# Time mixing of an RWKV layer: the gap of key and top, and the residual of the shift product, summed in PSUM by identity products

## The reference, cut to what matters

```
xs = shift x by one token;  xk = x*tm_k + xs*(1-tm_k)   (xv, xr likewise)
k = xk @ Wk.T;  v = xv @ Wv.T;  r = sigmoid(xr @ Wr.T)
per token t and channel (w: decay, u: time_first):
    q   = max(pp, k + u)
    e1  = exp(pp - q);  e2 = exp(k + u - q)
    wkv = (e1*aa + e2*v) / (e1*bb + e2)
    pp_new = max(pp - exp(w), k);  aa, bb carried on
out = x + (r * (layernorm(wkv)*ln_g + ln_b)) @ Wo.T
```

## Time and profile before

| | |
|---|---|
| median of 3 runs | 853.4 us (853.35 to 854.92) |
| the profiled execution | 852.91 us, its span 851.2 us |
| busy over the span | PE 649.4 us, PEld 534.9, DVE 541.4, ACT 342.6, POOL 327.1 |
| the time mixing's phase | from 447.3 to 617.7 us of the span |
| mean granted clock of PE | 0.878 of full speed |

### The profile page before, as it was taken

The page is one execution under the profiler, slowest core; times in us unless marked ns, Lnnn a source line. Parts: engine busy times, 40 slices in busy tenths (PEclk is TensorE's granted clock), DMA queues, the critical chain, the costliest instruction groups (busy, mean ns, idle before and its releaser), DMA issues. The chain is left out here.

```text
span 851.2 us, 14119 instructions
## 1 busy us (share of the span) xinstructions
PE 649.4 (76%) x4265; PEld 534.9 (63%) x4265; DVE 541.4 (64%) x1122; ACT 342.6 (40%) x760; POOL 327.1 (38%) x306
## 2 busy tenths in 40 slices
PE   4989999669916999999944899999344069999600
PEld 3656665358815888888833788888344048888400
DVE  4578989626782556444421799998556748888433
ACT  1567777324402333333315566544045025555200
POOL 5877764000003343434314466634310043331075
PEclk9999999969967999999986999999755569999855
DMA  4000000045303111111106000000059023332154
GB/s 124 1 2 1 2 2 2 3 149 189 95 1 87 52 56 57 57 57 50 50 25 198 1 1 1 2 0 1 0 180 307 8 67 98 99 100 81 50 152 138
DMA packets 38466, 54.23 MB, mean 64 GB/s; under 512 B 7252, under 2 KB 30422, under 8 KB 38262
## 3 DMA queue, kind: packets, MB, share of 16 engines
q1 hardware_dynamic: 31624, 34.80, 12.7%
q0 software_dynamic: 6768, 18.49, 7.3%
HBM read 37.28 MB, written 15.99 MB: 63 GB/s over the span
## 5 line engine op out<-in xcount | busy, mean ns | idle before, releaser
L1611 PE MATMUL banks<-r_xt,r_w_mixed 128*128 128x256 f32 x384 | 86.6, 385 | 1.4 <-ACT r_xt L1679 1.4
L1611 PEld LDWEIGHTS banks<-r_xt,r_w_mixed 128*128 128x128 f32 x384 | 73.1, 192 | 12.4 <-ACT r_xt L1679 2.1
L1357 DVE SCALAR_TENSOR_TENSOR f0x_s<-f0x_th,banks 128x512 f32<-128x512 f32 x35 | 24.1, 689 | 82.7 <-ACT f0x_th L1316 78.0
L1219 POOL DMA_INDIRECT f_y<-f0x_yout,f_slot_of x35 | 34.4, 983 | 102.1 <-ACT f0x_yout L1335 99.9
L1205 POOL DMA_INDIRECT f1x_xg<-f_xn,f_token_of x39 | 37.0, 948 | 75.5 <-PE banks L1256 50.9
L568 DVE TENSOR_REDUCE a_ssum<-a_e 128x6 f32<-128x1536 f32 x32 | 56.0, 1749 | 2.7 <-ACT a_e L454 2.5
L1272 PE MATMUL banks<-f_w_hi,f0x_xt_hi 128*128 x140 | 56.1, 401 | 0.2 <-issue 0.2
L1316 ACT ACTIVATE f0x_th<-banks 128x512 f32<-128x512 f32 x35 | 20.9, 598 | 86.5 <-PE banks L1272 86.5
L1272 PE MATMUL banks<-f_w_hi,f0x_xt_lo 128*128 x140 | 55.6, 397 | 0.0
L1272 PE MATMUL banks<-f_w_lo,f0x_xt_hi 128*128 x140 | 55.3, 395 | 0.0
L454 ACT ACTIVATE a_e<-banks 128x1536 f32<-128x1536 f32 x32 | 46.5, 1455 | 15.8 <-PE banks L351 15.8
(11 more groups left out here) (330 smaller groups left out, 1889.0 us busy)
## 6 DMA issues: line engine op xcount, KB each, us to landing
f_y<-f1x_yout SPq DMA_DIRECT2D x39, 128.0 KB
f0r_stage<-in_f_w13T SPq DMA_DIRECT2D x4, 1024.0 KB
r_y<-f_y SPq DMA_DIRECT2D x16, 256.0 KB, 6.0
f1r_stage<-in_f_w13T SPq DMA_DIRECT2D x8, 512.0 KB
f0r_stage<-in_f_w2T SPq DMA_DIRECT2D x4, 512.0 KB
f_xn<-f0r_xn SPq DMA_DIRECT2D x8, 256.0 KB
f1r_stage<-in_f_w2T SPq DMA_DIRECT2D x8, 256.0 KB
f_xn<-f1r_xn SPq DMA_DIRECT2D x8, 256.0 KB
```

The source lines that it names most:

```text
L1219: pool.indirect_dma_start(k.y_dram, bass.IndirectOffsetOnAxis(ap=k.slot_of[:, t:t + 1], axis=0), yout[:, t % YB, :], None).then_inc(scatte ...
L1611: last = pe.matmul(bank(1 + kind)[:, eb * T:(eb + 1) * T], r.w_mixed[:, kind, j // KB, j % KB, eb * P:(eb + 1) * P], xt[:, b % 2, j % KB, ...
```

## The change: what it does

Two sums that DVE did are made by PE in PSUM, as products with an identity matrix.

- The gap. `ku` and `dif` are gone. PE gets a step `gap(b)`, between `centre(b-1)` and `shift(b-1)`: for each half, k times the identity and top times minus the identity (`less_one`) are accumulated in bank 5, 4 products in all. It waits for `top_done(b)`. `clamp(b)` on ACT now reads bank 5, in halves, with `first` (u) as bias, or minus u (`less_first`) where the scale is -1: 4 instructions of 128 x 256 in place of 2 of 128 x 512. The two `ku` instructions of ACT and the one `dif` of DVE go.
- The residual. `shift(b-1)` adds x_res times the identity to each of its two groups, 2 products more. `add_shift(b-1)` moves from DVE to ACT: a Copy of bank 7 into x_res, no addition.
- Bank 5 is also where `deviate` writes, so `deviate(b-1)` also waits for `rel_done(b)`.
- DVE makes `less_one` (128 x 128) and `less_first` (128 x 2) once, in the expert phase before.

```
+  less_one = ident * -1;  less_first = first * -1          # DVE, once, in prepare(0)
 PE
+  def gap(self, b):
+      pe.wait_ge(done["top_done"], b + 1)
+      at_least(pe, done["ve_done"], b - 1)
+      for eb in range(EB):
+          pe.matmul(bank(5)[:, eb * T:(eb + 1) * T], m.ident[:], kt[:, 0, eb, 0:T], start=True, stop=False)
+          last = pe.matmul(bank(5)[:, eb * T:(eb + 1) * T], r.less_one[:], top[:, eb, 0:T], start=False, stop=True)
+      last.then_inc(done["dif_in"], 1)
   def shift(self, b):
+      pe.wait_ge(done["added"], b + 1)
       for s in range(S):
           for eb in range(EB):  pe.matmul(bank(7)..., s1..., r.wo_shift...)
+          last = pe.matmul(bank(7)[:, s * D:(s + 1) * D], m.ident[:], m.x_res[:, S * b + s, :],
+                           start=False, stop=True)
   def deviate(self, b):
+      pe.wait_ge(done["rel_done"], min(b + 2, B))
 ACT
   def products(self, b):
-      for eb in range(EB):
-          last = act.activation(ku[:, eb, :], bank(1)..., ACT.Identity, bias=r.first[:, eb:eb + 1])
+  def add_shift(self, b):
+      act.wait_ge(done["shifted"], b + 1)
+      act.activation(m.x_res[:, S * b:S * b + S, :], bank(7)..., ACT.Copy).then_inc(done["shift_added"], 1)
   def clamp(self, b):
-      act.activation(rel[:, 0], dif[:], ACT.Relu)
-      act.activation(rel[:, 1], dif[:], ACT.Relu, scale=-1.0).then_inc(done["rel_done"], 1)
+      for eb in range(EB):
+          act.activation(rel[:, 0, eb, :], gap, ACT.Relu, bias=r.first[:, eb:eb + 1])
+          last = act.activation(rel[:, 1, eb, :], gap, ACT.Relu, bias=r.less_first[:, eb:eb + 1], scale=-1.0)
 DVE
-  def gap(self, b):        dve.tensor_tensor(dif[:], ku[:], top[:, :, 0:T], ALU.subtract)
-  def add_shift(self, b):  dve.tensor_tensor(two, two, bank(7)..., ALU.add)
```

More of the change, by code:

```diff
@@ L1396, in prepare @@
                     dve.tensor_scalar(r.grown[:], r.grown[:], -1.0, None, ALU.mult)
+                    dve.tensor_scalar(r.less_one[:], m.ident[:], -1.0, None, ALU.mult)
+                    dve.tensor_scalar(r.less_first[:], r.first[:], -1.0, None, ALU.mult)
                 elif 1 <= n <= 3 * KB:
@@ L1464, in rwkv_memory @@
     r.mean_of, r.cen_same, r.cen_other = sb("mean_of", [P, P]), sb("cen_same", [P, P]), sb("cen_other", [P, P])
+    r.less_one, r.less_first = sb("less_one", [P, P]), sb("less_first", [P, EB])
     return r
@@ L1478, in rwkv_phase @@
     xt = sb("xt", [P, 2, KB, T + 1])
-    kt, ku, vs = sb("kt", [P, 2, EB, T + 1]), sb("ku", [P, EB, T]), sb("vs", [P, EB, T])
+    kt, vs = sb("kt", [P, 2, EB, T + 1]), sb("vs", [P, EB, T])
     th, s1 = sb("th", [P, EB, T]), sb("s1", [P, 2, EB, T])
     less, sc, ab = sb("less", [P, 2, EB, T]), sb("sc", [P, 3, EB, T]), sb("ab", [P, 2, EB, T + 1])
-    dif, rel, ex = sb("dif", [P, EB, T]), sb("rel", [P, 2, EB, T]), sb("ex", [P, 2, EB, T])
+    rel, ex = sb("rel", [P, 2, EB, T]), sb("ex", [P, 2, EB, T])
     e2v, e1a, num, den, rden, wkv, sq, rw = (
@@ L1487, in rwkv_phase @@
     names = ("edges first_weighed second_weighed first_added added stats_done mv_done ve_in_done root_done neg_mean_ready "
-             "xn_ready xt_in_psum xt_ready r_done k_done v_done th_done s1_done k_ready ku_ready v_ready "
-             "top_done less_done sc_done dif_done rel_done ex_done f2v_done e2v_done scan_done e1a_done num_done "
+             "xn_ready xt_in_psum xt_ready r_done k_done v_done th_done s1_done k_ready v_ready "
+             "top_done less_done sc_done dif_in rel_done ex_done f2v_done e2v_done scan_done e1a_done num_done "
              "e1b_done den_done rden_done wkv_done centred sq_done rw_done shifted shift_added var_done ve_done rstd_done "
@@ L1606, in products @@
                 pe.wait_ge(done["xt_ready"], b + 1)
-                for kind, free, made in ((2, "th_done", "r_done"), (0, "ku_ready", "k_done"), (1, "v_ready", "v_done")):
+                for kind, free, made in ((2, "th_done", "r_done"), (0, "k_ready", "k_done"), (1, "v_ready", "v_done")):
                     at_least(pe, done[free], b)
@@ L1631, in shift @@
                     for eb in range(EB):
-                        last = pe.matmul(bank(7)[:, s * D:(s + 1) * D], s1[:, b % 2, eb, s * P:(s + 1) * P],
-                                         r.wo_shift[:, eb, :], start=(eb == 0), stop=(eb == EB - 1))
+                        pe.matmul(bank(7)[:, s * D:(s + 1) * D], s1[:, b % 2, eb, s * P:(s + 1) * P],
+                                  r.wo_shift[:, eb, :], start=(eb == 0), stop=False)
+                    last = pe.matmul(bank(7)[:, s * D:(s + 1) * D], m.ident[:], m.x_res[:, S * b + s, :],
+                                     start=False, stop=True)
                 last.then_inc(done["shifted"], 1)
@@ L1691, in products @@
                 at_least(act, done["less_done"], b)
+                at_least(act, done["dif_in"], b)
                 act.activation(k_in, bank(1).rearrange("p (e t) -> p e t", e=EB), ACT.Copy).then_inc(done["k_ready"], 1)
-                at_least(act, done["dif_done"], b)
-                for eb in range(EB):
-                    last = act.activation(ku[:, eb, :], bank(1)[:, eb * T:(eb + 1) * T], ACT.Identity, bias=r.first[:, eb:eb + 1])
-                last.then_inc(done["ku_ready"], 1)
                 act.wait_ge(done["v_done"], b + 1)
@@ L1709, in grow @@
                 act.activation(sc[:, 1:3], less[:], ACT.Exp).then_inc(done["sc_done"], 1)
+            def add_shift(self, b):
+                act.wait_ge(done["shifted"], b + 1)
+                act.activation(m.x_res[:, S * b:S * b + S, :], bank(7).rearrange("p (s c) -> p s c", s=S),
+                               ACT.Copy).then_inc(done["shift_added"], 1)
             def clamp(self, b):
-                act.wait_ge(done["dif_done"], b + 1)
-                act.activation(rel[:, 0], dif[:], ACT.Relu)
-                act.activation(rel[:, 1], dif[:], ACT.Relu, scale=-1.0).then_inc(done["rel_done"], 1)
+                act.wait_ge(done["dif_in"], b + 1)
+                for eb in range(EB):
+                    gap = bank(5)[:, eb * T:(eb + 1) * T]
+                    act.activation(rel[:, 0, eb, :], gap, ACT.Relu, bias=r.first[:, eb:eb + 1])
+                    last = act.activation(rel[:, 1, eb, :], gap, ACT.Relu, bias=r.less_first[:, eb:eb + 1], scale=-1.0)
+                last.then_inc(done["rel_done"], 1)
                 act.wait_ge(done["rel_done"], b + 1)
@@ L1741, in scores @@
                 dve.wait_ge(done["k_ready"], b + 1)
+                at_least(dve, done["dif_in"], b)
                 for eb in range(EB):
@@ L1748, in scores @@
                                   ALU.subtract).then_inc(done["less_done"], 1)
[L1750 to L1753, removed]
             def scan(self, b):
@@ L1784, in gate @@
                 dve.tensor_tensor(flat(rw[:]), bank(4), flat(s1[:, b % 2]), ALU.mult).then_inc(done["rw_done"], 1)
[L1786 to L1789, removed]
             def vary(self, b):
```

## The result

| | before | after |
|---|---|---|
| median | 853.38 us (4 runs, 851.93 to 854.92) | 868.18 us (4 runs, 866.09 to 871.4) |
| ratio | | 1.0177, 95% interval 1.014 to 1.0213 |
| profiled execution, its span | 852.91, 851.2 us | 866.09, 864.3 us |
| from the first turn's start to the start of `var_eps`, the phase's last DVE instruction | 157.25 us (457.34 to 614.59) | 173.52 us (454.80 to 628.32) |
| turn to turn, mean of sequences 3 to 7 | 17.09 us | 19.48 us |

The kernel is slower by 1.8%. The first turn started anywhere from 454.8 to 458.3 us in the traces of this study, in code that hardly differs.

The account below looks back on a forecast made before the run. PE was taken as the bound, with about 0.2 us slack per iteration; steps of +0.1, +1.8, +12.3, +0.6 and +0.87 made +15.6 us, giving 868.5 to 869.0, forecast 868.8, range 866 to 872.5.

Parts of the forecast that it names:

- (a): Phase start, gap(0) between turn(1) and products(1): mostly absorbed by PE's old wait, centre(0) 0.1 us later.
- (b): From centre(0) to products(2): gap(1) newly waits for top(1)'s scan; products(2) start 1.8 us later.
- (c): Five periods from products(2) to products(7): 97.5 us after against 85.23 before, +12.3 us.
- (d): Last iteration: vary(6) on DVE waits for the later deviate(6), +0.6 us, making +14.7 together.
- (e): Behind wkv(7), where nothing overlaps: shift(7) holds two more products, +0.87 us, making +15.6 together.
- The lower price, at the transposes' pace: Rival: identity products on PE cost 1.30 us per iteration, not 2.61, giving 860 us; chance 0.05.
- the weight loads' free 13%: Rival: PE's weight loads leave 2.2 us per period free, hiding 2.2 of 2.61; time near 856 us; chance 0.01.
- What the prediction took at nothing: DVE's later path, deviate's wait for rel_done, ACT's copy, new PE waits, two expert-phase instructions: each costed at nothing.
- The signs that were named: Middle turns 19.5 us apart without PE idling, DVE idle some 4 us, products(7) near 592, vary(6) waiting, span near 867.
- What DVE loses hides behind PE: Each iteration: DVE loses dif and the residual's addition, 0.685 and 0.688 us, with no gain because PE is the bound.
- I let the clock fall as before: Tail, PE's wait for wkv(7): clock assumed to fall again; if it held, the end would come 1.6 us earlier.

Follow-up runs that it names:

- the first of those three: Kernel before, with ACT scaling and POOL adding the inputs for k and v, so PE needs 4 products each, not 8; 861.76 us, ratio 1.0098.

## Why the prediction was right

The forecast was 868.8 with a range of 866 to 872.5; 868.18 was measured. By its steps, in distances from the first turn:

| step | predicted | measured |
|---|---|---|
| (a) until centre(0) | +0.1 | +0.02 (26.76 to 26.78) |
| (b) until products(2) | +1.8 | +1.85 (35.51 to 37.38, less a) |
| (c) until products(7) | +12.3 | +12.15 (120.74 to 134.76) |
| (d) until centre(7) | +0.6 | +0.48 (145.14 to 159.64) |
| (e) until vary(7) | +0.87 | +2.13 (152.96 to 169.59) |
| from there to `var_eps` | 0 | -0.36 |
| phase | +15.6 | +16.27 |

In the last row but one DVE waits 0.36 us less for POOL's root (0.88 and 1.23); why isn't shown.

The mechanism, that the changed kernel goes by PE's work at 0.43 to 0.44 us per product, is shown from two sides: products without a use, added to the kernel before, give the same period of 19.48, and in the changed kernel DVE's two instructions can be put back while the period stays at 19.48. The lower price, at the transposes' pace, is excluded by the starts in the changed kernel's iteration, 0.43 apart. That the weight loads' free 13% is room for new products is excluded as well: the loads are busy 17.64 of 20 us after the change and 17.46 before, and the new products cost their full price. What the prediction took at nothing in the phase cost nothing there: DVE has 4.2 us of waits per iteration, and no wait of PE's ends with rel_done.

The signs that were named came too: turns 19.48 us apart, DVE idle 4.21 us, a wait of vary(6) for deviate(6) of 0.44. products(7) started at 589.56 and not near 592, and the span is 864.3 and not 867, since the first turn began 2.54 us earlier.

One sentence of the mechanism was wrong without a price. "What DVE loses hides behind PE" holds for the changed kernel. In the kernel before, DVE's relief would have gone into its wait for POOL in any case, since DVE's ring through ACT and POOL takes 17.00 us with the two instructions or without. The 0.1 to 0.2 us per iteration that PE waited were waits for rw, which comes out of this ring.

The mis-sized term is (e). I let the clock fall as before, which it did, and took the stretch behind it to cost as before plus the two products. It cost more, because the clock doesn't rise at a fixed time after the first product. The rise came 5.7 us after centre(7)'s start and not 3.2, and 1.26 us more were paid. With the wait filled, the phase falls by 2.80, which is what centre and shift lost at the lower clock (7.24 against 4.42).

That the total came so close, 868.8 against 868.18, is partly luck. In the profiled executions the phase grew by 0.67 us more than reckoned, but the stretch ahead of it was 2.54 us shorter and the one behind it 0.55, so that the changed one took 866.09 where 868.5 was reckoned; the median of the runs lies 2.1 above that execution. By medians the difference is 14.8, with an interval of 1.4 to 2.1%, which is 12 to 18 us, and the reckoned 15.6 and the phase's 16.27 both lie in it. Why the stretch before the first turn varies by some 3 us between executions stays open. What the additions to DVE's list there cost can't be read from it.

## What to carry to other kernels

Before work is moved between two nearly full engines, ask which of them has room where the work is to go: PE had 0.1 to 0.2 us in 17, and each float32 product of 256 columns with the identity costs as much as a real one (0.436 us). Moving an elementwise addition of 0.69 us to PE cost 0.87 us there for the residual and 1.74 for the gap. The test is cheap in both directions: products that nobody reads on the one, and the instructions left out on the other.

Ask as well whether the engine that is relieved would be faster for it. DVE was busy 95% of the time, but the two instructions stood in a stretch where it would otherwise have waited for ACT and POOL, and without them it waited (0.52 us became 1.88).

## What the runs showed of the hardware that I had not expected

- Additions and products of two 128x512 tensors on DVE took 0.69 us alone and 1.65 to 1.73 beside POOL's additions and products of two tensors, ending 0.55 behind POOL's. In the kernel before only wkv showed a trace of it (0.95 where POOL ran beside it, 0.69 where it didn't). The reciprocal of the same size, with one input, took 3.35 in every sequence of the kernel before and of the first of those three, with POOL's products beside it. Work given to POOL isn't free for DVE.
- PE's clock fell 4.1 us after the end of the last product in the kernel before and 4.6 in the changed one. In another run it fell during new products, 0.8 us after they had begun behind 2.27 us of idle time, and in one with the same products behind 2.28 us of idle time it didn't fall. It rose 3.2 us after the start of centre(7) in one kernel and 5.7 in the other. The place of the change is not fixed by the last or first product alone.
